# A Mamba-style scan with its output and gate turned to channels in rows, and the orders of five engines rewritten

## Chip, cores and metric

One NeuronCore of one Trainium2 chip. The metric is device time in microseconds (us) of the whole program, the median of several runs.

## The reference

For 32 sequences of 512 tokens with 256 channels, x becomes x + norm(attn(norm(x))) and then x + norm(ffn(norm(x))). All is fp32. The part called attn is a state-space scan:

```
q = rope(x @ W_in[:256].T); h = rmsnorm(q) * w
z, xBC, dt = split(h @ W_zxbcdt.T)            # 512, 768 and 8 columns
dt = softplus(dt + dt_bias)                   # 8 heads of 64 channels
x_ssm, B, C = split(silu(causal_conv4(xBC)))  # 512, 128 and 128
y = scan(x_ssm, dt, A, B, C) + D * x_ssm
y = rmsnorm(y * silu(z)) * w2
out = y @ W_out.T + q
```

The scan works in chunks: within a chunk y = (C B^T * decay) (x dt), and across chunks through a state of 128 x 64 for each head. The kernel uses chunks of 128 tokens. The part called ffn is a mixture of 16 experts of width 64 with a router, and a shared expert of width 512.

## The kernel before

The work of one sequence is cut into parts: p (first norm, q, rope, h by channel), a (projections, convolution, scan, output projection, residual), f (router, gates, ups, downs of the feed-forward) and g (final norm, store). An iteration of the loop does part a of sequence i, part p of sequence i+1, part f of sequence i-1 and the end of i-2, interleaved. Five engines run their own programs and meet only at semaphores. The order of each is written out by hand in the functions first, iteration, tail and drain of each engine's block: SP at 534 to 551, POOL (GpSimd) at 699 to 730, ACT (ScalarE) at 950 to 1002, DVE (VectorE) at 1336 to 1381, PE (TensorE) at 1659 to 1715. The loop runs iteration for i from 2 to 30; lead, first and iteration(1) stand ahead of it, tail, drain and last behind it.

PSUM has three banks for part a (apb), one for p (ppb), two for f (fpb) and two for the down projection (acc). PLANS lists in which order banks are filled, and which engine fills a name's reader and which frees it; slot() on PE waits until the bank's last user is done.

A product that must be nearly fp32 exact is done in split form: operands are rounded to a high part (fp32r) and a low rest, and split_mm (L1443) sends three matmuls for each block of 128 input channels: high x high, high x low and low x high. Matmuls within the scan take plain fp32 operands. narrow (L1492, L1494) does the same for few output columns, with tokens as the stationary operand: two matmuls for each block of 128 tokens and 128 channels.

The steps that the change touches, in order for chunk c of 128 tokens:

- project_z(c, n) puts z by token into PSUM, in halves a and b of 256 columns. The a half carries dt's 8 columns too (264). dt_bias_add(c) (L1112) reads them; silu_z (L855) writes zs, tokens in rows. decays, cumulate (L1518 to L1520) and evac_acs make the cumulated decays; SP stores them as rows to memory and loads them back replicated to all partitions (decay_rows), POOL masks them (L607), ACT takes their exp (exp_seg, L845), DVE multiplies them by C B^T (decay_CB, L1167), all in seg.
- x_by_token(c) transposes the convolved x (L1452). times_dt(c) makes xdt = x dt (L1159) and xD = D x (L1162).
- diagonal(c) (L1575): for each of 8 heads one matmul with seg (128 x 128) as the stationary operand and 64 columns of xdt streaming. Its output yd has tokens in rows.
- from_state(c) (L1560): C as the stationary operand, 512 columns of the state S streaming. state_part(c) (L1173) scales it by the decay of each token (ea). chunk_y(c) (L1191) adds the two. state(c) (L1567) and new_state(c) update S.
- gated(c) on POOL (L622, L623): y = (xD + chunk y) * zs.
- y_by_channel(c) transposes y in 4 pieces (L1452, ident with zs). evac_y (L867) and y_low (L1228) split it into yTh and yTl. square_y (L872) sums the squares of each token.
- project_out(t) is the output projection; mixed_out, add_x and norm_x1 (L881) finish the residual and normalise it for the feed-forward. ffn_by_channel (L1462, from xdt) transposes that at the start of the next iteration.

```
for h in range(HS):
    hs = slice(h * PD, (h + 1) * PD)
    ins = nc.tensor.matmul(b[:, hs], seg[:, c % 2, h, :], xdt[:, c % 2, hs], start=True, stop=True)
```

## Time and profile before

| | |
|---|---|
| median of 3 runs | 3193.36 us (3184.57 to 3193.8) |
| profiled execution | 3187.6 us; span from first to last instruction 3185.9 us |
| busy, of the span | PE 98%, PEld (weight loads) 85%, DVE 75%, ACT 61%, POOL 64% |
| share of PE in the chain that ended last | 95% |
| mean granted clock of TensorE | 0.989 of 2.4 GHz |

Busy time of PE is the union of records that overlap: a matmul's record ends when its last result is out, while the next has begun. The time that one costs is from its start to the next one's start. PEld are the loads of stationary operands, which can run ahead of the matmuls.

### The profile page before, as it was taken

Reading aid. Unit: us, or ns where it says so; the run is one execution under the profiler, and the core shown is the slowest. Engines: PE = TensorE matmul, PEld = TensorE weight load, DVE = VectorE, ACT = ScalarE, POOL = GpSimd, SP = SyncE. Lnnn points to the kernel's source line nnn. Section 1 sums busy time; section 2 is a strip of 40 time slices with the busy share of each in tenths; the row PEclk is TensorE's granted clock in tenths of the full one; section 3 lists DMA queues with packets and bytes.
Section 4 is the critical chain, followed back from the end, with each engine's and each line's share of the span. In section 5 each row is a group of like instructions: output and inputs, shape, how many; then the busy total and the mean of one; then the engine's idle time right before and its main releaser. Section 6 shows DMA issues by size and latency. Waiting matters only on the chain.

```text
span 3185.9 us, 62383 instructions
## 1 busy us (share of the span) xinstructions
PE 3112.3 (98%) x19648; PEld 2722.1 (85%) x19648; DVE 2394.2 (75%) x5104; ACT 1935.2 (61%) x4149; POOL 2031.2 (64%) x2311
## 2 busy tenths in 40 slices
PE   5899999999999999999999999999999999999997
PEld 4688888888888888888888888888888888888886
DVE  5877877777777777777777777778777777777763
ACT  5565666665666556666566666656656656665562
POOL 2477666677666676656676666776666776666764
PEclk7899999999999999999999999999999999999999
DMA  3123222222222222222122222222222222222222
GB/s 123 41 68 87 73 73 67 66 66 85 73 64 64 71 73 76 80 66 58 64 86 76 76 60 66 66 86 73 73 66 66 66 86 73 64 67 69 73 74 48
DMA packets 143433, 227.33 MB, mean 71 GB/s; under 512 B 18976, under 2 KB 88352, under 8 KB 143392
## 3 DMA queue, kind: packets, MB, share of 16 engines
q1 hardware_dynamic: 126496, 210.06, 20.1%
q0 software_dynamic: 16896, 16.78, 4.0%
q8 instruction: 20, 0.33, 0.0%
q14 instruction: 21, 0.17, 0.0%
HBM read 174.87 MB, written 35.13 MB: 66 GB/s over the span
## 4 chain that ended last, share of the span: by engine, by line
PE 95%; DVE 0%; POOL 0%; ACT 0%; issue 0%; ACTq 0%; DVEq 0%; POOLq 0%
PE fpb L1443 34%; PE apb L1443 20%; PE acc L1629 17%; PE apb L1575 7%; PE apb L1452 4%; PE ppb L1443 3%; PE apb L1560 3%; PE apb L1567 2%; PE ppb L1462 2%; PE apb L1547 1%; PE fpb L1492 1%; PE fpb L1462 1%; PE fpb L1494 1%; PE fpb L1608 0%; PE apb L1520 0%; PE apb L1519 0%
## 5 line engine op out<-in xcount | busy, mean ns | idle before, releaser
L652 POOL TENSOR_TENSOR hidL<-hid,hidH 128x512 fp32r<-128x512 f32 x384 | 544.9, 1419 | 234.8 <-ACT hidH L914 226.8
L1130 DVE SCALAR_TENSOR_TENSOR xc<-apb,cw,xc 128x511 f32<-128x511 f32 (+2 forms) x576 | 427.8, 747 | 63.9 <-ACT xc L827 35.9
L1629 PE MATMUL acc<-WDH,hidH 128*128 128x256 f32 x1536 | 456.7, 297 | 4.4 <-POOLq L654 4.4
L914 ACT CAST hidH<-hid 128x512 fp32r<-128x512 f32 x384 | 236.2, 615 | 341.9 <-POOL hid L647 283.6
L1629 PE MATMUL acc<-WDH,hidL 128*128 128x256 f32 x1536 | 431.4, 281 | 0.0
L1629 PE MATMUL acc<-WDL,hidH 128*128 128x256 f32 x1536 | 430.9, 281 | 0.0
L647 POOL TENSOR_TENSOR hid<-hid,cb 128x512 f32<-128x512 f32 x256 | 347.5, 1358 | 73.2 <-DVEq L1251 42.1
L1249 DVE TENSOR_TENSOR hid<-hid,fpb 128x512 f32<-128x512 f32 x384 | 261.1, 680 | 135.6 <-PE fpb L1443 132.3
L1443 PE MATMUL fpb<-fTh,UH 128*128 128x512 f32 x768 | 335.7, 437 | 0.0
L845 ACT ACTIVATE seg<-seg,acs 128x128 f32<-128x128 f32 x1024 | 313.6, 389 | 11.5 <-ACT cb L895 5.7
L1443 PE MATMUL fpb<-fTh,GH 128*128 128x512 f32 x768 | 318.6, 415 | 0.0
L1629 PEld LDWEIGHTS acc<-WDH,hidH 128*128 128x128 f32 x1536 | 289.9, 189 | 19.9 <-issue 7.4
L1443 PE MATMUL fpb<-fTh,GL 128*128 128x512 f32 x768 | 304.1, 396 | 0.0
L1443 PE MATMUL fpb<-fTh,UL 128*128 128x512 f32 x768 | 303.9, 396 | 0.0
L903 ACT ACTIVATE hid<-fpb 128x512 f32<-128x512 f32 x384 | 228.5, 595 | 123.2 <-PE fpb L1443 83.9
L1443 PE MATMUL fpb<-fTl,UH 128*128 128x512 f32 x768 | 302.5, 394 | 0.0
L1443 PE MATMUL fpb<-fTl,GH 128*128 128x512 f32 x768 | 302.5, 394 | 0.0
L1629 PEld LDWEIGHTS acc<-WDL,hidH 128*128 128x128 f32 x1536 | 290.1, 189 | 12.7 <-issue 7.2
L1629 PEld LDWEIGHTS acc<-WDH,hidL 128*128 128x128 f32 x1536 | 289.7, 189 | 0.0
L1575 PEld LDWEIGHTS apb<-xdt,seg 128*128 128x128 f32 x2048 | 246.7, 194 | 11.9 <-issue 6.6
L1575 PE MATMUL apb<-xdt,seg 128*128 128x64 f32 x2048 | 246.1, 274 | 2.9 <-DVE seg L1167 2.8
L1167 DVE TENSOR_TENSOR seg<-seg,CBs 128x1024 f32<-128x1024 f32 x128 | 198.4, 1550 | 43.6 <-ACT seg L845 34.1
(195 smaller groups left out, 8669.6 us busy)
## 6 DMA issues: line engine op xcount, KB each, us to landing
seg<-acs_row SPq DMA_DIRECT2D x128, 512.0 KB, 4.2
cb<-c_row SPq DMA_DIRECT2D x512, 128.0 KB, 2.9
xsP<-in_x SPq DMA_DIRECT2D x32, 512.0 KB, 3.6
xc<-qrot SPq DMA_DIRECT2D x32, 512.0 KB, 3.4
xc<-in_x SPq DMA_DIRECT2D x32, 512.0 KB, 4.3
out<-xc SPq DMA_DIRECT2D x32, 512.0 KB, 3.0
out<-xn POOLq DMA_DIRECT2D x32, 512.0 KB, 6.0
ZL_loaded<-in_wzx_t SPq DMA_DIRECT2D x2, 512.0 KB, 4.4
```

Source lines behind the costliest of these rows:

```text
L647: G.tensor_tensor(hid[:, j % 2, :], hid[:, j % 2, :], cb[:, r % 2, :], ALU.mult).then_inc(sem["routed_ready"], 1)
L652: own.do(G.tensor_tensor(hidL[:, j % 2, :], hid[:, j % 2, :], hidH[:, j % 2, :].bitcast(fp32), ALU.subtract))
L845: ins = A.activation(seg[:, c % 2, h, :], seg[:, c % 2, h, :], ACT.Exp, bias=acs[:, 0, c * HS + h:c * HS + h + 1])
L903: own.do(A.activation(hid[:, j % 2, :], way.bank(f"G{j}")[:], ACT.Silu))
L914: A.copy(hidH[:, j % 2, :], hid[:, j % 2, :]).then_inc(sem["hidden_high"], 1)
L1130: ins = V.scalar_tensor_tensor(xc[:, b, s:], src[:, 0:T - s], cw[:, b, TAPS - 1 - s:TAPS - s], xc[:, b, s:], ALU.mult, ALU.add)
L1167: V.tensor_tensor(seg[:, c % 2, :, :], seg[:, c % 2, :, :], CBs[:, c, :].unsqueeze(1).broadcast_to([P, HS, P]), ALU.mult).then_inc(sem["m_ ...
L1249: own.do(V.tensor_tensor(hid[:, j % 2, :], hid[:, j % 2, :], way.bank(f"U{j}")[:], ALU.mult))
L1443: ins = nc.tensor.matmul(dst, l, r, start=n == 0, stop=n == total - 1)
L1452: ins = nc.tensor.transpose(b[:, t * P:(t + 1) * P], src(t), ident[:])
L1575: ins = nc.tensor.matmul(b[:, hs], seg[:, c % 2, h, :], xdt[:, c % 2, hs], start=True, stop=True)
L1629: ins = nc.tensor.matmul(dst, l[:, w, tk], r[:, j, :], start=j == 0 and t % 2 == 0 and n == 0, stop=j == HB - 1 and n == 2, skip_group_che ...
```

## The change

The scan's output and z are kept with channels in rows and tokens along the row, so that y need not be transposed before the output projection.

- project_z(j) now has the weights of 128 channels as the stationary operand and 512 tokens streaming: four groups of six matmuls. dt gets a weight tile of its own, DTW, and project_dt, by narrow, for all 512 tokens. dt_bias_add takes all chunks at once.
- diagonal(c): 64 columns of xdt are the stationary operand and the 128 columns of seg stream. Even heads write partitions 0 to 63 and odd heads 64 to 127.
- from_state(c): four matmuls with a block of 128 columns of S as the stationary operand and C's 128 columns streaming.
- The decay of a token now varies along the row. own_rows on SP loads the decay rows of chunks 1 to 3 a second time, two heads to a block of channels, into own_decay (128 x 1536), which overlays xTh and xTl; row_exp on ACT takes their exp. state_part multiplies by them. ea is gone.
- xD = D x is made from xc in SBUF with D by channel (dcol).
- y_by_channel is gone. evac_y and y_low read zs. A single yTh/yTl pair is kept, which now has its own semaphores (yT_read, out_begun).
- The squares' sum runs over partitions now: square_y writes squares, sum_squares on DVE adds four blocks to one, squares_by_token on PE multiplies by a column of ones, squares_out copies to ssy.
- The orders of all engines and the plans of all stages are new, with more switches of ACT's function tables (exp_table, silu_table) in iteration: five pairs where there were three.

```diff
-            def project_z(c, n):
...
-                fill(name, split_mm(b[:, 0:cs.stop - cs.start], [(hTh[:, k, tk], hTl[:, k, tk], ZH[:, k, cs], ZL[:, k, cs])
-                                                                 for k in range(KD)],
-                                    sem["hT_read"] if c == NT - 1 and n == 1 else None))
+            def project_dt():
+                b = slot("dt")
+
+                pe.wait_ge(s_hT, 2)
+                pe.sem_inc(s_hT, -2)
+                fill("dt", narrow(b, hTh, hTl, DTW, HS))
+
+            def project_z(j):
+
+                name, lo = f"z{j}", j * P + (HS if j >= NB // 2 else 0)
+                cs = slice(lo, lo + P)
+                fill(name, split_mm(slot(name)[:], [(ZH[:, k, cs], ZL[:, k, cs], hTh[:, k, :], hTl[:, k, :])
+                                                    for k in range(KD)], sem["hT_read"] if j == NB - 1 else None))
...
-                fill(f"yo{c}", nc.tensor.matmul(b[:], xc[:, 5, c * P:(c + 1) * P], S[:], start=True, stop=True))
+                for j in range(NB):
+                    js = slice(j * P, (j + 1) * P)
+                    ins = nc.tensor.matmul(b[:, js], S[:, js], xc[:, 5, c * P:(c + 1) * P], start=True, stop=True)
+                fill(f"yo{c}", ins)
...
-                    hs = slice(h * PD, (h + 1) * PD)
-                    ins = nc.tensor.matmul(b[:, hs], seg[:, c % 2, h, :], xdt[:, c % 2, hs], start=True, stop=True)
+
+                    half = slice(h % 2 * PD, (h % 2 + 1) * PD)
+                    ins = nc.tensor.matmul(b[half, h // 2 * P:(h // 2 + 1) * P], xdt[:, c % 2, h * PD:(h + 1) * PD],
+                                           seg[:, c % 2, h, :], start=True, stop=True)
...
-            def y_by_channel(c):
-                b = slot(f"yT{c}")
-                pe.wait_ge(sem["yg_ready"], c + 1)
-                fill(f"yT{c}", transposes(b, lambda j: zs[:, c, j * P:(j + 1) * P], NB))
+            def squares_by_token(s):
+                b = slot(f"ss{s}")
+                for n in range(2):
+                    c = 2 * s + n
+                    pe.wait_ge(sem["qs_ready"], c + 1)
+                    ins = nc.tensor.matmul(b[:, n:n + 1], junk[n][:, 0:P], ones[:, 0:1], start=True, stop=True)
+                fill(f"ss{s}", ins)
...
+            def own_rows():
+
+                sp.wait_ge(sem["acs_stored"], 16)
+                for a in range(2):
+                    sp.dma_start(own_decay[a * PD:(a + 1) * PD, :, :],
+                                 rows(acs_row, [[0, PD], [2 * P, (NT - 1) * NB], [1, P]], (HS + a) * P)
+                                 ).then_inc(sem["ear_loaded"], 16)
...
+            def row_exp():
+                act.wait_ge(sem["ear_loaded"], 32)
+                A.activation(own_decay[:], own_decay[:], ACT.Exp).then_inc(sem["ear_ready"], 1)
...
+            def sum_squares(c):
+
+                dve.wait_ge(sem["sq_ready"], c + 1)
+                q = junk[c % 2]
+                own.do(V.tensor_tensor(q[:, 0:2 * P], q[:, 0:2 * P], q[:, 2 * P:4 * P], ALU.add))
+                V.tensor_tensor(q[:, 0:P], q[:, 0:P], q[:, P:2 * P], ALU.add).then_inc(sem["qs_ready"], 1)
```

The new order of PE in the loop (iteration; "if g" lines in place):

```
project_dt(); ffn_by_channel(0); project_x(4); ffn_by_channel(1); project_z(0); project_x(5); down(10)
logits(0); down(11); logits(1); cumulate(); project_x(0); gate(0); project_x(1); up(0); project_x(2)
gate(1); project_z(1); gate(2); project_x(3); up(1); gate(3); project_z(2); up(2); project_z(3); CB()
B_by_token(); down(0); x_by_token(0); up(3); x_by_token(1); down(1); combine_by_expert(); state(0)
gate(4); diagonal(0); x_by_token(2); down(2); up(4); down(3); gate(5); from_state(1); state(1); up(5)
gate(6); diagonal(1); from_state(2); state(2); up(6); down(4); diagonal(2); x_by_channel(0); gate(7)
x_by_token(3); up(7); down(5); squares_by_token(0); project_out(0); from_state(3); project_q(0)
diagonal(3); gate(8); down(6); up(8); x_by_channel(1); project_out(1); gate(9); project_q(1); down(7)
project_out(2); up(9); squares_by_token(1); gate(10); h_by_channel(0); project_out(3); down(8); up(10)
down(9); h_by_channel(1); gate(11); up(11)
```

## Rows read from the trace of the kernel before

**Rows 1.** Windows, one period: length, then busy PE, PEld, DVE, ACT, POOL, clock, DMA.
```profile
1500.00:1596.40 96.40, 96.36 (x616) 84.52 (x615) 74.14 (x160) 59.79 (x129) 63.31 (x74) 1.00 0.23 71
```
**Rows 2.** The chain of waits in order of time: start, length, piece, records.
```profile
1514.81 1.73 PE apb L1575 x16
...
1559.33 2.79 PE fpb L1443 x12
...
1588.54 0.71 PE apb L1443 x6
...
1611.20 1.73 PE apb L1575 x16
```
**Rows 3.** Timeline of PE: start, length of the group's records, line, form, records.
```profile
1503.85 1.05 PE L1547 MATMUL apb<-xc 128*128 128x128 f32 x8
1504.73 0.60 PE L1452 MATMUL apb<-ident,xc 128*128 128x128 f32 x4
```
**Rows 4.** Timeline of PE around diagonal(0).
```profile
1514.64 1.89 PE L1575 MATMUL apb<-xdt,seg 128*128 128x64 f32 x16
...
1516.66 0.39 PE L1443 MATMUL fpb<-fTl,UH 128*128 128x512 f32 x1
```
**Rows 5.** Timeline of PE around the transposes of y, chunk 0.
```profile
1528.25 0.60 PE L1452 MATMUL apb<-ident,zs 128*128 128x128 f32 x4
...
1528.92 0.39 PE L1443 MATMUL fpb<-fTl,GH 128*128 128x512 f32 x1
```
**Rows 6.** Timeline of PE around the router's product, first and last of 16 records.
```profile
1576.10 0.18 PE L1492 MATMUL fpb<-R,fTh 128*128 128x32 f32 x1
...
1577.69 0.26 PE L1494 MATMUL fpb<-R,fTl 128*128 128x16 f32 x1
1577.80 0.37 PE L1443 MATMUL apb<-ZH,hTh 128*128 128x264 f32 x1
1578.00 0.28 PE L1443 MATMUL apb<-ZL,hTh 128*128 128x264 f32 x1
```
**Rows 7.** Timeline of PE around from_state(1).
```profile
1517.83 1.02 PE L1560 MATMUL apb<-S,xc 128*128 128x512 f32 x2
1518.68 1.02 PE L1567 MATMUL apb<-xdec,Btok 128*128 128x512 f32 x2
```
**Rows 8.** Timelines of PE and DVE at the loop's boundary.
```profile
1566.83 0.40 PE L1443 MATMUL fpb<-fTh,UL 128*128 128x512 f32 x1
1567.27 0.36 PE L1443 MATMUL apb<-ZH,hTh 128*128 128x264 f32 x1
...
1566.47 0.69 DVE L1107 TENSOR_TENSOR hTl<-ppb,hTh 128x512 fp32r<-128x512 f32 x1
```
**Rows 9.** Timelines of PE and PEld around cumulate.
```profile
1589.09 0.30 PE L1518 MATMUL apb<-ad,upper 128*128 128x32 f32 x2
...
1589.55 0.41 PE L1520 MATMUL apb<-upper,ad 128*32 128x128 f32 x2
...
1590.22 0.39 PE L1443 MATMUL fpb<-fTl,GH 128*128 128x512 f32 x1
...
1589.20 0.30 PEld L1519 LDWEIGHTS apb<-ad,ones 128*128 128x128 f32 x2
1589.54 0.14 PEld L1520 LDWEIGHTS apb<-upper,ad 128*32 128x32 f32 x2
```
**Rows 10.** Groups of weight loads by form: busy us, mean ns of one, idle before.
```profile
L1518 PEld LDWEIGHTS apb<-ad,upper 128*128 128x128 f32 x64 | 10.1, 192 | 2.2 <-ACT xc L832 2.1
...
L1520 PEld LDWEIGHTS apb<-upper,ad 128*32 128x32 f32 x64 | 4.4, 109 | 1.3
```
**Rows 11.** Groups of ScalarE by form.
```profile
L765 ACT ACT_TABLE_LOAD x98 | 125.7, 1283 | 6.5 <-ACT hid L903 5.3
...
L855 ACT ACTIVATE zs<-apb 128x256 f32<-128x256 f32 x256 | 94.4, 382 | 25.0 <-PE apb L1443 13.7 <-ACT hid L903 8.1 <-DVE dr L1112 2.7
```
**Rows 12.** Timelines of ACT and PE at norm_x1(1) and ffn_by_channel(1).
```profile
1568.64 1.09 ACT L881 ACTIVATE xdt<-xc,nb,rstd 128x256 f32<-128x256 f32 x2
...
1570.64 0.60 PE L1462 MATMUL fpb<-ident,xdt 128*128 128x128 f32 x4
```

More of the change, by code:

```diff
@@ L242, in build @@
+            "drain": Plan({
                 "f": (
@@ new lines, in iteration @@
+                squares_by_token(0); project_out(0); from_state(3); project_q(0); diagonal(3); gate(8)
+                settled("m_ready"); down(6); up(8); x_by_channel(1); project_out(1); settled("xn_ready")
+                gate(9); project_q(1); down(7); settled("p_out_DVE"); project_out(2); up(9)
+                squares_by_token(1); gate(10); settled("a_out_DVE", "qs_ready"); h_by_channel(0)
+                project_out(3); settled("p_out_ACT"); down(8); settled("yl_ready"); up(10); down(9)
@@ new lines, in tail @@
+                logits(1); gate(0); B_by_token(); up(0); cumulate(); project_z(1); settled("ad_ready")
+                project_x(0); gate(1); project_x(1); gate(2); project_x(2); up(1); CB(); project_x(3); gate(3)
+                up(2); project_z(2); project_z(3); up(3); down(0); settled("acc_free"); x_by_token(0)
+                x_by_token(1); down(1); combine_by_expert(); gate(4); settled("c_ready"); state(0); up(4)
+                diagonal(0); gate(5); from_state(1); state(1); x_by_token(2); down(2); up(5); down(3); gate(6)
@@ new lines, in tail @@
+                state(2); diagonal(1); down(4); settled("xdec_ready"); from_state(2); up(6); gate(7); down(5)
+                x_by_token(3); from_state(3); up(7); settled("a_out_ACT"); diagonal(2); gate(8); down(6)
+                project_out(0); squares_by_token(0); up(8); gate(9); diagonal(3); project_out(1)
+                settled("m_ready"); down(7); up(9); gate(10); project_out(2); squares_by_token(1); down(8)
+                settled("a_out_DVE", "qs_ready"); up(10); project_out(3); gate(11); settled("f_out_ACT")
```

522 lines of the change are left out of this document (262 added, 260 removed).

## Prediction

> **What bounds the kernel now.** I read the busy table by windows first. One stretch of 96.40 us of the loop has TensorE busy for 96.36, VectorE for 74.14, ScalarE for 59.79 and GpSimd for 63.31, at the full clock (2.4 GHz) [rows 1]. The chain of waits gives the period: the first diagonal product of one iteration begins at 1514.81 and that of the next at 1611.20, so a sequence takes 96.4 us [rows 2]. 29 loop iterations make 2796 of the 3187.6 us. The profiled execution took 3187.6 (span 3185.9); the median of the three runs is 3193.36, which is 5.8 above it.
>
> "Busy" says little on TensorE, since its records overlap. I cost by start to start instead. A 512-column matmul of a split product takes 2.79/12 = 0.233 us, a 256-column one 0.71/6 = 0.118 [rows 2]. Full fp32 matmuls appear as two records each. With a 128-column stationary operand each record costs 0.111, whether 128 or 64 columns stream: B·C takes 0.88/8 = 0.110 [rows 3]; the diagonal product takes 1516.66 - 1514.64 - 0.233 = 1.79 for 16 records, 0.112 each [rows 4]. So the old diagonal product is bound by its weight loads. I add up TensorE's work per sequence, since nothing else fills the period.
>
> **What leaves and what comes, in TensorE time per sequence.**
>
> - *Transposes of y* (4 groups, L1452 with zs) go. One costs 1528.92 - 1528.25 - 0.233 = 0.44 [rows 5], so -1.76.
> - *z*: 24 matmuls of 256 columns and 24 of 264 become 24 of 512. Without the 8 extra columns (24 x 8 at 2.4 GHz is 0.08) the old ones take 48 x 0.118 = 5.66; in all 5.74 against 24 x 0.233 = 5.59: -0.15.
> - *dt* becomes a product of its own, of the same form as the router's: 16 matmuls with 128-column stationary operands. The router's take 1578.00 - 1576.10 - 0.12 = 1.78 [rows 6]. So +1.78: eight columns carried along almost free are now paid for with 16 weight loads.
> - *Sums of squares by token*: four fp32 matmuls with one streamed column, 8 records x 0.111 = +0.89.
> - *from_state*: one 512-column matmul, 1518.68 - 1517.83 = 0.85 [rows 7], becomes four of 128 columns, as B·C does at 0.88. Three times 0.03: +0.09.
> - *Loop boundary*: the last matmul of up(11) starts at 1566.83 and the first z at 1567.27 instead of 1567.06, because VectorE's second half of hTl runs from 1566.47 to 1567.16 [rows 8]. The exposed weight load after it adds 0.08. In the new order gate(11) and up(11), 2.8 us, follow h_by_channel(1) instead of 1.4, which covers this: -0.29.
>
> These sum to +0.56. All hang on the order holding, since TensorE has no gaps to fill.
>
> - *Diagonal product.* Before, 4 x 1.79 = 7.16. The stationary operand is now 64 columns of xdt and 128 columns stream. No row of before has two halves of the array in use, so I bound it. Above: one after another, a 128-column fp32 record streams twice, 256 columns at 2.4 GHz = 0.107, x16 = 1.71. Below: heads in different halves run side by side. Each head has two records in its own half, in order, so the last of one head overlaps the first of the next: 8.5 steps x 0.107 = 0.91. Weight loads permit this: one of 128 columns lasts 0.192 and one of 32 lasts 0.109 [rows 10], 0.00086 per column, so 64 columns issue about every 0.055, and 16 x 0.055 = 0.88.
> - *Entering and leaving a narrow stationary operand.* cumulate has one (L1520, 32 columns). From 1589.09 to 1590.22 less 0.233 is 0.90 for its six records, where 4 x 0.111 + 2 x 0.107 = 0.66 would do; the gap lies before and after L1520 [rows 9]. So 0.24 an excursion, four of them; with the wider exposed load I take 0.26. Bound below: nothing, as the 16-column combine transposes fit in ordinary time.
>
> I take side by side: 4 x (0.91 + 0.26) = 4.68, so -2.48. The row nearest to it is L1520: two loads there end 0.14 us after the first begins, against 0.30 for two wide ones [rows 9], and the array drains around them, as if it was set up differently for a narrow operand. Such a setup would be the one that has halves.
>
> A page bears on this from both sides. "TensorE: Matmul & The Clock Gate" of the Trainium skill, section "Part 3: Packing small matmuls", gives 2.38x for three column tiles; at that efficiency two tiles gain 1.59x, as an estimate, and the product would be 1.08 + 0.26. No run shows it yet.
>
> Sum: +0.56 - 2.48 = -1.92, a period of 94.5.
>
> **Other engines.** ScalarE loses eight silus of 0.382 [rows 11], the accumulator reads and one small exp; it gains four silus twice as long, an exp of 128x1536 (at most 6 x 0.382 = 2.3), and four table loads, five pairs a sequence for three, at 1.283 [rows 11] = 5.1. It ends near 65 to 66 of 94.5. VectorE gains about 3 (two short additions for each chunk, two copies), near 77. GpSimd keeps its work. All are below TensorE. SP gets two more row loads of 0.4 MB and issues decay_rows(1) ahead of decay_rows(0). Nothing that the first masks need stands behind the new loads, and from cumulate to diagonal(0) TensorE now has about 28 us of other work (14 projections, gates and ups of 1.4, and nine smaller groups); queued behind them are the prefetch of the next x, the combine rows and decay_rows(2), none needed within 10 us. The halves of x by channel, xTh and xTl, now share memory with own_decay: evac_xT(0) waits for chunk_y(2), which ends before it, as exp_seg(3) stands ahead of it on ScalarE.
>
> **Where lateness would show.** The tightest distance I find is the loop-carried one: project_out(3) to ffn_by_channel(1). Before, the second normalisation ends on ScalarE at 1568.64 + 1.09 = 1569.73 and its transposes start at 1570.64, so 0.9 in hand [rows 12]. The distance is 11.5 before, and after (down 1.42, up 1.40, down 1.42, transposes 0.44, gate and up 2.80, dt 1.78, transposes 0.44, xc4 1.40) it is 11.1: 0.5 left. The transposes head TensorE's in-order queue, so each further microsecond costs one per sequence. Next comes the new round trip square_y(3), sum_squares(3), squares_by_token(1), squares_out(1), root_y(1), mixed_out(1); its TensorE part stands 13 us after diagonal(3), and chunk_y, gated, gate(9), square, mixed_out(0) and rope(1) take about 11 of them. I allow 0.2 per sequence for such waits: -1.7.
>
> Over 31 sequences (the loop, iteration 1 and the tail; lead, first and drain I hold equal) that is -53, or 3135 against the profiled 3187.6. The runs lie on average 3 above it (two near 3193, one at 3184.6), and the after's median should as well: 3139.
>
> **Rivals.**
>
> 1. *The halves don't overlap.* Each diagonal product costs 1.71 + 0.26 = 1.97: 4 x 1.97 - 7.16 = +0.72, with +0.56 and no waits +1.28, x31 = +40: 3230, slower. This decides above 1.60 a product (there the sum with the 0.2 is zero). For it: every row of TensorE shows starts in order and at least a stream apart. Against it: the drain around L1520. Chance 0.19.
> 2. *Loads of a half aren't hidden behind the other half's matmul.* 16 x (0.055 + 0.107) + 0.26 = 2.85 each, +4.8 a sequence: 3340. Against it: the second load of L1520 is hidden. Chance 0.04. The same section of the Trainium skill speaks for this one: it says that a load overlaps a running matmul only in another row group, and all heads here use all rows.
> 3. *Lateness.* The halves overlap but the loop-carried chain or the squares' round trip keeps TensorE waiting 1 us or more a sequence: 3160 to 3190; at 1.9 the gain is gone. For it: 0.5 us in hand, ten table loads on ScalarE, more hops. Against: the before's orders show almost no idle time at all. Chance 0.10.
> 4. *Forecast*, 0.67. Its own range goes from 3105 (no drain cost: 4 x 0.26 x 31 = 32 less) to 3165 (the product at 1.4, +0.23 each, or waits of 0.9).
>
> **Numbers.** The range takes in the forecast's low end and rival 1 with the runs' spread: 3105 to 3235. That leaves out rival 2, parts of rivals 1 and 3, and a product cheaper still. Faster by over 0.3%, which is about what a measurement of this kernel tells from no change (10 us): 0.67 and most of rival 3, less a little for the ends: 0.71. Within 0.3%: 0.06. Slower: 0.23.
>
> **What would show it.** In the profile after: a period near 94.7; diagonal groups of 16 records in about 1.2 us with pairs of starts far less than 0.1 apart (rival 1: even steps of 0.107); gaps of 0.1 on both sides of each group; the dt group at 1.78; no idle time of TensorE before ffn_by_channel(1). A wait of TensorE on xdt's normalisation, or on the squares, would show rival 3. The forecast fails on the product's price before all else, since it alone turns the sign.

## The result and the profile after

The changed kernel takes 3356.43 us (median of 4, 3353.89 to 3359.7), the kernel before in the same job 3189.96: a ratio of 1.0524, 95% interval 1.0502 to 1.0545. The forecast was 3139 and faster. The profiled execution took 3357.49 us (span 3355.8).

The page of the kernel after, busy time and then the chain that ended last, by engine:

```profile
PE 3168.5 (94%) x19712; PEld 2702.9 (81%) x19712; DVE 2623.1 (78%) x5362; ACT 2138.6 (64%) x4015; POOL 2123.5 (63%) x2311
...
DVE 34%; PE 33%; ACT 10%; POOL 10%; issue 9%; DMA 3%; DVEq 0%; POOLq 0%; ACTq 0%; PEldq 0%; SPq 0%
```

TensorE, which held 95% of the chain before, now holds 33%, and VectorE as much: a new wait, not more work. A period was 96.4 us. It is now 102.1 in four iterations of five and 100.1 in the fifth. One of the short ones, the windows view of after (columns as in [rows 1]):

```profile
1052.50:1152.70 100.20, 95.67 (x619) 81.50 (x618) 81.19 (x167) 65.28 (x124) 66.52 (x72) 1.00 0.28 76
```

TensorE was busy for all but 0.04 us of its period in [rows 1]; here 4.5 are idle. ScalarE (65.3) is where the forecast put it, VectorE is 81.2 instead of 77. Who TensorE waited for over the whole run of after (total us, times, longest):

```profile
PE apb L1638 <- DVE xdec L1271: 71.0, 31, 2.3
PE ppb L1513 <- DVE xn L1112: 21.7, 32, 4.7
PE ppb L1497 <- DVE xTl L1092: 13.1, 10, 2.1
PE apb L1543 <- issue: 10.9, 30, 0.4
```

L1638 is squares_by_token and L1271 the second addition of sum_squares. Timeline of PE, after:

```profile
1081.99 0.40 PE L1497 MATMUL fpb<-fTh,GL 128*128 128x512 f32 x1
1082.31 1.09 PE L1629 MATMUL apb<-seg,xdt 128*64 128x128 f32 x16
1083.34 0.66 PE L1505 MATMUL apb<-ident,xc 128*128 128x128 f32 x4
...
1106.27 0.28 PE L1638 MATMUL apb<-ones,xc 128*128 128x1 f32 x2
1108.87 0.38 PE L1638 MATMUL apb<-ones,xdec 128*128 128x1 f32 x2 [2.33 <-DVE xdec L1271]
...
1140.65 0.40 PE L1497 MATMUL fpb<-fTh,UL 128*128 128x512 f32 x1
1141.41 0.25 PE L1543 MATMUL apb<-DTW,hTh 128*128 128x16 f32 x1 [0.36 <-issue]
```

Three things are to be read here. The 16 records of the diagonal product take 1082.31 to 1083.34, 1.03 us where before's take 1.70 (the 1.79 of [rows 4] takes in 0.08 of the step behind the group, from 1516.35 to 1516.66): the halves run side by side. Ahead of the group there is 0.09 more (0.32 from the last wide matmul instead of 0.233), and something behind it; experiment 1 gives the whole price. The sums of squares begin at 1106.27 and then stand for 2.3 us. And the loop's boundary has grown: 1140.65 to 1141.41 is 0.76, where [rows 8] had 0.44.

What VectorE did while TensorE stood, timelines of DVE and of POOL, after:

```profile
1103.49 0.62 DVE L1270 TENSOR_TENSOR xc<-xc 128x256 f32<-128x256 f32 x1 [0.24 <-DVE hid L1300]
1104.14 0.29 DVE L1271 TENSOR_TENSOR xc<-xc 128x128 f32<-128x128 f32 x1
...
1105.36 0.77 DVE L1263 TENSOR_TENSOR yTl<-zs,yTh 128x512 fp32r<-128x512 f32 x1 [0.33 <-DVE xdt L1219]
1106.06 1.49 DVE L1270 TENSOR_TENSOR xdec<-xdec 128x256 f32<-128x256 f32 x1
1107.58 1.24 DVE L1271 TENSOR_TENSOR xdec<-xdec 128x128 f32<-128x128 f32 x1
...
1105.54 1.72 POOL L634 TENSOR_TENSOR xD<-xD,xdt 128x512 f32<-128x512 f32 x1
1107.34 1.32 POOL L636 TENSOR_TENSOR zs<-zs,xD 128x512 f32<-128x512 f32 x1
```

The same two additions take 0.62 and 0.29 for chunk 0 and 1.49 and 1.24 for chunk 1, and each of the long ones ends just after a GpSimd instruction does (1107.55 after 1107.26, 1108.82 after 1108.66). Over the run, the 57 second additions that began with GpSimd idle took 0.291 to 0.294; the 71 that began under a running instruction had a median of 1.265, and their length follows what was left of it (correlation 0.98).

GpSimd waits too. Its 512-column operations that begin while VectorE has no operation under way on two SBUF sources take 1.28 (the low halves of hid, L665, median). The 157 on two sources that began under VectorE's seg<-seg,CBs, S<-S,el or y_low last 1.12 to 1.16 plus what was left of VectorE's operation (correlation 0.999): the 1.72 above began under y_low, which ends at 1106.13. So each engine's delay feeds the other's. Groups of DVE by form, after:

```profile
L1263 DVE TENSOR_TENSOR yTl<-zs,yTh 128x512 fp32r<-128x512 f32 x128 | 122.8, 959 | 22.7 <-DVE xdt L1219 17.2 <-ACT yTh L883 5.4
L1178 DVE TENSOR_TENSOR xD<-xc,dcol 128x512 f32<-128x512 f32 x128 | 106.2, 830 | 0.0
L1271 DVE TENSOR_TENSOR xdec<-xdec 128x128 f32<-128x128 f32 x64 | 82.7, 1292 | 2.2
...
L1201 DVE TENSOR_TENSOR own_decay<-apb,own_decay 128x512 f32<-128x512 f32 x96 | 65.6, 683 | 12.2 <-PE apb L1612 11.5 <-DVE ssy L1275 0.3 <-DVE xdt L1219 0.3
```

and of the kernel before:

```profile
L1178 DVE TENSOR_TENSOR S<-S,el 128x512 f32<-128x512 f32 x64 | 92.0, 1438 | 0.5 <-DVE xdt L1191 0.2
L1228 DVE TENSOR_TENSOR yTl<-apb,yTh 128x512 fp32r<-128x512 f32 x128 | 87.6, 685 | 18.1 <-ACT yTh L867 10.5 <-DVE xdt L1191 7.4
L1162 DVE TENSOR_TENSOR xD<-apb,dbc 128x512 f32<-128x512 f32 x128 | 86.9, 679 | 0.0
```

Where one source is a PSUM bank (apb), 512 columns take 0.68 us in both kernels. Where both are in SBUF they take 0.83, 0.96, 1.44 in the mean. y_low and xD were of the first kind and have become the second; sum_squares is new and of the second. With y_low this costs GpSimd as well: its operations that began under y_low have a median of 1.28 in the kernel before and of 1.71 after. The row S<-S,el was there to be read before the forecast.

That a VectorE operation with two SBUF inputs and a GpSimd instruction exclude each other is what the Trainium skill says ("SBUF — State Buffer", section "Who interferes with whom": such an instruction "contends with a GpSimd instruction that reads SBUF", the later one waits for the other's end, and tensor_reduce never contends on trn2). The trace agrees in the additions, in the waits of GpSimd and in the rows with one PSUM source; the reduction is tried below.

Last, the clock. Windows of after: from the start of the dt product (1039.62) on, and around the squares of the iteration before (TensorE is idle for 2.35 us within the third line, 2.48 busy of 4.83):

```profile
1039.62:1042.46 2.84, 2.84 (x23) 2.75 (x24) 0.49 (x1) 1.94 (x4) 2.62 (x6) 1.00 0.28 99
1042.46:1045.87 3.41, 3.41 (x12) 2.73 (x11) 1.08 (x4) 1.75 (x3) 2.57 (x3) 0.50 0.00 0
...
1003.50:1008.33 4.83, 2.48 (x23) 2.40 (x22) 4.46 (x6) 3.57 (x7) 2.91 (x2) 1.00 0.00 0
1008.33:1011.74 3.41, 3.41 (x19) 3.41 (x18) 2.41 (x4) 2.12 (x4) 2.41 (x3) 0.50 0.68 229
```

A granted clock of 0.50 is 1.2 GHz. Iterations of 102.1 us have two such stretches of 3.41 us, those of 100.1 none: one begins 0.7 to 1.8 us after TensorE's wait at the squares has ended, the other 1.9 to 3.0 us after the dt product has begun. Over the run they make 229.9 us, where the kernel before had 69.7, all of it outside 400 to 3000 us.

### The profile page after: what moved, and what is told of

Its sections match the earlier page's. It is cut to its first block, busy times and chain, and to the rows that moved or that the text cites. A ratio compares the mean times of both kernels' runs of the same rounds, so it can differ in the third digit from the quotient of the medians.

```text
span 3355.8 us, 63442 instructions
## 1 busy us (share of the span) xinstructions
PE 3168.5 (94%) x19712; PEld 2702.9 (81%) x19712; DVE 2623.1 (78%) x5362; ACT 2138.6 (64%) x4015; POOL 2123.5 (63%) x2311
## 4 chain that ended last, share of the span: by engine, by line
DVE 34%; PE 33%; ACT 10%; POOL 10%; issue 9%; DMA 3%; DVEq 0%; POOLq 0%; ACTq 0%; PEldq 0%; SPq 0%
PE apb L1497 10%; PE fpb L1497 8%; DVE xc L1144 6%; PE acc L1689 5%; ACT seg L856 4%; POOL hidL L665 3%; DVE hid L1300 3%; DMA out<-xn 3%; DVE xdec L1271 2%; ACT L777 2%; DVE st L1080 2%; DVE yTl L1263 2%; PE ppb L1497 2%; DVE xc L1270 2%; DVE S L1206 2%
## 5 line engine op out<-in xcount | busy, mean ns | idle before, releaser
L665 POOL TENSOR_TENSOR hidL<-hid,hidH 128x512 fp32r<-128x512 f32 x384 | 531.8, 1385 | 452.4 <-ACT hidH L928 436.8
L1144 DVE SCALAR_TENSOR_TENSOR xc<-apb,cw,xc 128x511 f32<-128x511 f32 (+2 forms) x576 | 430.7, 748 | 66.1 <-ACT xc L840 37.5
L1689 PE MATMUL acc<-WDH,hidH 128*128 128x256 f32 x1536 | 445.0, 290 | 3.1 <-POOLq L667 3.1
L1497 PE MATMUL fpb<-fTh,GH 128*128 128x512 f32 x768 | 327.7, 427 | 0.0
L917 ACT ACTIVATE hid<-fpb 128x512 f32<-128x512 f32 x384 | 228.3, 595 | 108.4 <-PE fpb L1497 94.2
L1497 PE MATMUL apb<-hTh,ZH 128*128 128x512 f32 x640 | 275.5, 430 | 3.5 <-ACT xc L845 3.5
L1497 PE MATMUL apb<-hTl,ZH 128*128 128x512 f32 x640 | 264.3, 413 | 0.0
L1497 PE MATMUL apb<-hTh,ZL 128*128 128x512 f32 x640 | 263.9, 412 | 0.0
```

Of the source, the lines that this page charges most:

```text
L665: own.do(G.tensor_tensor(hidL[:, j % 2, :], hid[:, j % 2, :], hidH[:, j % 2, :].bitcast(fp32), ALU.subtract))
L917: own.do(A.activation(hid[:, j % 2, :], way.bank(f"G{j}")[:], ACT.Silu))
L1144: ins = V.scalar_tensor_tensor(xc[:, b, s:], src[:, 0:T - s], cw[:, b, TAPS - 1 - s:TAPS - s], xc[:, b, s:], ALU.mult, ALU.add)
L1497: ins = nc.tensor.matmul(dst, l, r, start=n == 0, stop=n == total - 1)
L1689: ins = nc.tensor.matmul(dst, l[:, w, tk], r[:, j, :], start=j == 0 and t % 2 == 0 and n == 0, stop=j == HB - 1 and n == 2, skip_group_che ...
```

## The experiments

All ratios are to the kernel before on the same chip; its median lay between 3186.3 and 3190.5 in every job. "Period" is from cumulate to cumulate.

**1. The diagonal product alone, on the kernel before.** `b1_halves` turns it round with heads in alternating halves, `b2_one_half` puts heads 0 to 3 in one half and 4 to 7 in the other. Both leave the layout of y as it comes, so the output isn't the reference's.

```diff
-   ins = nc.tensor.matmul(b[:, hs], seg[:, c % 2, h, :], xdt[:, c % 2, hs], start=True, stop=True)
+   half = slice(h % 2 * PD, (h % 2 + 1) * PD)        # b2_one_half: h // 4
+   ins = nc.tensor.matmul(b[half, h // 2 * P:(h // 2 + 1) * P], xdt[:, c % 2, h * PD:(h + 1) * PD],
+                          seg[:, c % 2, h, :], start=True, stop=True)   # b2_one_half: h % 4
```

> The kernel before with the diagonal product alone turned round: 64 columns of xdt as the stationary operand, seg streaming, even and odd heads in the two halves of the partitions. Nothing behind it is adapted, so y has the wrong layout: only the time is read. In the trace of the changed kernel such a product takes 1.03 us for its 16 records, 1.1 with what it adds around it, against 1.79. If that price holds by itself and TensorE is still the bound: 4 x 0.69 x 32 = 88 us less, about 3102. If the price in the changed kernel only came from TensorE having waited before it, no change: 3190.

> As the one before, but heads 0 to 3 go to one half and heads 4 to 7 to the other, so that neighbours in the order share a half (the layout of y is again not the reference's). If the gain comes from two halves running side by side, this has none: 15 steps of 0.107 and 0.2 around them, 1.8 to 1.9 a product, 3190 to 3205. If it comes from the smaller stationary operand (loads of 64 columns), this is as fast as the alternating one, about 3102.

`b1_halves`: 3129.56 (3127.3 to 3132.4), 0.9816 (0.9796 to 0.9836), periods of 94.2 and 94.6. `b2_one_half`: 3177.14, 0.9966 (0.9955 to 0.9976), period 96.1. The product in each, timelines of PE, first of `b1_halves`:

```profile
1392.20 0.28 PE L1443 MATMUL apb<-ZH,hTl 128*128 128x256 f32 x1
1392.41 1.09 PE L1575 MATMUL apb<-seg,xdt 128*64 128x128 f32 x16
1393.43 0.51 PE L1443 MATMUL fpb<-fTh,UH 128*128 128x512 f32 x1
1393.78 0.40 PE L1443 MATMUL fpb<-fTl,UH 128*128 128x512 f32 x1
```

and of `b2_one_half`:

```profile
1412.72 1.58 PE L1575 MATMUL apb<-seg,xdt 128*64 128x128 f32 x16
1414.23 0.50 PE L1443 MATMUL fpb<-fTh,UH 128*128 128x512 f32 x1
```

1.02 against 1.51: most of the gain comes from heads in different halves next to each other, and it is worth 57 us by itself. The change's central idea holds; the loss comes from the rest. Both expectations missed in size. In `b2_one_half` the starts within a half are 0.109 apart, as expected, but the seven steps around the one change of half (heads 3 and 4) are 0.055 in the mean, which I had not counted. And 3102 was too low because the price of 1.1 left out what stands behind the group. Counted as in [rows 4], up to the second matmul behind it, the product costs 1393.78 - 1392.20 - 0.118 - 0.233 = 1.23, where [rows 4] has 1.79. That is 0.56 less, four times 2.24, and the shorter period is 2.22 below before's 96.4. The longer one has 0.4 more, at two steps inside the down and z products. The changed kernel's product by the same count costs 1.22.

**2. The additions.** `a1_reduce` lets VectorE sum the four blocks with one operation (ACT writes the squares so that the four to be summed lie side by side). `a2_no_adds` leaves the sum out and copies one column in its place.

```diff
-   own.do(V.tensor_tensor(q[:, 0:2 * P], q[:, 0:2 * P], q[:, 2 * P:4 * P], ALU.add))
-   V.tensor_tensor(q[:, 0:P], q[:, 0:P], q[:, P:2 * P], ALU.add).then_inc(sem["qs_ready"], 1)
+   V.reduce_sum(q[:, 0:P], q.rearrange("p (n j) -> p n j", j=NB), AX.X).then_inc(sem["qs_ready"], 1)
...
-   A.activation(junk[c % 2].rearrange("p (j n) -> p j n", j=NB), zs[:, :, c * P:(c + 1) * P], ACT.Square
+   A.activation(junk[c % 2].rearrange("p (n j) -> p j n", j=NB), zs[:, :, c * P:(c + 1) * P], ACT.Square
```

> The changed kernel with sum_squares as one reduction instead of two additions (the squares are written interleaved, so that it reads four neighbours for each sum); the same orders, the same result. Theory: VectorE's additions with both sources in SBUF wait until GpSimd's running instruction ends, take 7.1 us a sequence where 2.8 would do, and this makes VectorE late for squares_by_token, project_q(1) and h_by_channel(1). A reduction has one source and should not wait: about 0.65 x 4 = 2.6 a sequence, the wait at squares_by_token(0) falls from 2.4 to under 0.5, and the time to 3200 to 3260. Rival, the orders themselves are too tight (ScalarE's table loads, chunk y of chunk 2): the waits move elsewhere, 3330 or more.

> The changed kernel without the sum over the four blocks of squares: a copy of one column stands in for both additions, so the mean square is that of a quarter of the channels. The bound of what sum_squares can cost. Theory: 3190 to 3240, with no wait at squares_by_token(0). Rival, tight orders: 3320 or more.

`a1_reduce`: 3198.28 (3195.29 to 3204.34), 1.0038 (1.0026 to 1.005), period 96.05, and 97.6 in every third or fourth iteration; 97.1 us at half speed. `a2_no_adds`: 3187.77, 1.0007 (0.9995 to 1.0019). The edit of `a1_reduce`, the reduction and the order in which ScalarE writes the squares, carries 158 of the 167 us. Both times lie just below the range given for them. Groups of DVE and waits of TensorE, `a1_reduce`:

```profile
L1270 DVE TENSOR_REDUCE xdec<-xdec 128x128 f32<-128x512 f32 x64 | 43.0, 672 | 0.1
...
PE apb L1504 <- DVE xD L1178: 17.6, 30, 4.0
PE ppb L1512 <- DVE xn L1112: 11.8, 32, 4.7
```

The reduction takes 0.67 whether GpSimd runs or not (0.669 to 0.689 over 128). Per sequence that is 2.7 us of VectorE, against 7.1 for the additions, which alone would be 2.8. But VectorE's busy time of a period falls only from 81.2 to 79.3: in the new phase S<-S,el takes 1.72 in the mean for 1.24, seg 1.71 for 1.38 and y_low 1.22 for 0.96, all on two SBUF sources. Laid side by side at full clock, the periods of 100.14 (after) and 96.04 differ in TensorE's waits: squares_by_token(0) +2.47, project_q(1) +1.30 (for x_low(1), which VectorE does behind sum_squares(2)), h_by_channel(1) +0.46, four of 0.06 to 0.12, and x_by_token(2) -0.55.

**3. Where the squares are read, and whether they are awaited.** `a3_ss_later` moves squares_by_token(0) behind project_out(0); `a6_not_awaited` keeps both additions, but TensorE takes the fourth block of the squares, as ScalarE left it, and leaves out the others.

```diff
-   squares_by_token(0); project_out(0); from_state(3); ...          # a3_ss_later
+   project_out(0); squares_by_token(0); from_state(3); ...
...
+   dve.sem_inc(sem["qs_ready"], 1)                                  # a6_not_awaited
    own.do(V.tensor_tensor(q[:, 0:2 * P], ...))
-   V.tensor_tensor(q[:, 0:P], q[:, 0:P], q[:, P:2 * P], ALU.add).then_inc(sem["qs_ready"], 1)
+   own.mark(V.tensor_tensor(q[:, 0:P], q[:, 0:P], q[:, P:2 * P], ALU.add))
```

> The changed kernel with one step of TensorE's order moved in the steady iteration: the sums of squares by token of the first half stand behind project_out(0) (1.4 us of work) instead of ahead of it. Theory (VectorE's additions finish late because they are held up by GpSimd; the place in the order only decides how much of it TensorE sees): the 2.4 us that TensorE waits there shrinks to about 1.0, project_out(0) is ready on its own, and the period falls by about 1.4 from 102.1, perhaps 2 if a stretch at half speed shortens: 3290 to 3320. Rival (the place in the order is the whole fault): the wait vanishes and with it the stretches at half speed, period 96 to 97, 3200. Rival (the wait is for something else that comes at the same time): no change, 3357.

> The changed kernel with both additions on VectorE kept in their places, but TensorE takes only the fourth block of the squares and doesn't wait for them (three blocks are left out of the sum). This parts the additions' time on VectorE from the wait for their result. Theory (both count: the result comes late, and 7 us of VectorE time make x_low, norm_q and others behind them late): the 2.4 us wait goes, the period falls to about 98 and the stretches at half speed get rarer; 3220 to 3270. Rival A (only the round trip of the squares costs): 3190, as without the additions. Rival B (only VectorE's load costs): 3350.

`a3_ss_later`: 3297.12, 1.0331 (1.0306 to 1.0356), periods from 98.8 to 102.0, near what the theory had; at full clock 1.3 us less than after's 100.1. The wait has become two, of 0.8 at the squares and of 1.06 at from_state(3). `a6_not_awaited`: 3357.07, 1.0527 (1.0508 to 1.0545), no gain at all: my theory gave 3220 to 3270, and rival B, VectorE's load alone, was right. Waits of TensorE, `a6_not_awaited`:

```profile
PE apb L1613 <- DVEq L1055: 61.1, 30, 2.1
PE ppb L1514 <- DVE xn L1112: 23.5, 33, 4.7
PE ppb L1498 <- DVE xTl L1092: 22.7, 18, 2.6
```

The 2.3 us wait has moved, as one of 2.1, to from_state(3), whose bank is that of xt3, and times_dt(3), which frees it, stands right behind sum_squares(1) on VectorE. The wait named in the table was only the first of several for the same late engine.

**4. The suspected cost put into the kernel before.** `b3_adds` puts the two additions, on data that nobody reads, behind chunk_y four times a sequence; `b4_reduce` one reduction in each place.

```diff
    dve.sem_inc(sem["y_ready"], 1)                                   # end of chunk_y
+   for _ in range((0, 2, 1, 1)[c]):
+       own.do(V.tensor_tensor(ysp[:, 0:2 * P], ysp[:, 0:2 * P], ysp[:, 2 * P:4 * P], ALU.add))
+       own.do(V.tensor_tensor(ysp[:, 0:P], ysp[:, 0:P], ysp[:, P:2 * P], ALU.add))
...
+       own.do(V.reduce_sum(ysp[:, 0:P], ysp.rearrange("p (n j) -> p n j", j=4), AX.X))   # b4_reduce
```

> The kernel before with the suspected cost put in: the same two additions (256 and 128 columns, both sources in SBUF) four times a sequence, on data that nobody reads, in VectorE's order right behind chunk_y (twice behind that of chunk 1, once behind 2 and 3). Nobody waits for their result, only for what stands behind them on VectorE. Theory (VectorE has no room in time around the chunks, though it is busy for 74 of 96.4 us only, so work of its own there delays TensorE): 2.8 us of work and up to 4 us of waiting for GpSimd become 2 to 5 us of period: 3250 to 3340. Rival (the orders of before have room on VectorE, and only the changed kernel's orders have not): within 0.3% of 3190.

> The kernel before with one reduction (128 x 512 to 128 x 128, about 0.68 us) in each of the four places where the additions stood in the run before, on the same data that nobody reads. Own time on VectorE 2.7 us a sequence, as that of the additions alone (2.8). Theory (the additions cost by waiting for GpSimd, the reduction doesn't wait): 2.7 of VectorE time instead of 6.2, period 96.4 to 97.5, 3190 to 3225. Rival (any 2.7 us of work at these places makes VectorE late): 3303 as with the additions.

`b3_adds`: 3302.87, 1.0359 (1.0344 to 1.0374), period 99.65. `b4_reduce`: 3204.41, 1.0051 (1.0036 to 1.0067), period 96.5 and, in a third of the iterations, 96.9. Groups of DVE, `b3_adds`:

```profile
L1199 DVE TENSOR_TENSOR ysp<-ysp 128x128 f32<-128x128 f32 x128 | 101.0, 789 | 4.4
L1198 DVE TENSOR_TENSOR ysp<-ysp 128x256 f32<-128x256 f32 x128 | 96.5, 754 | 24.1 <-DVE xdt L1191 23.0
```

and `b4_reduce`:

```profile
L1198 DVE TENSOR_REDUCE ysp<-ysp 128x128 f32<-128x512 f32 x128 | 87.8, 686 | 24.0 <-DVE xdt L1191 22.9
```

This is the plainest pair. The own time is nearly the same (the additions 0.29 + 0.43 with GpSimd idle, four times: 2.9; the reduction 2.7). With its waiting the first comes to 6.2 us a sequence. The first costs 116 us and the second 18, in a kernel whose VectorE was busy for 74 of 96.4 us.

**5. GpSimd's instructions cut in four.** `a7_pool_pieces` is the changed kernel with GpSimd's 512-column operations on two sources in pieces of 128 columns.

```diff
-   own.do(G.tensor_tensor(hidL[:, j % 2, :], hid[:, j % 2, :], hidH[...].bitcast(fp32), ALU.subtract))
+   for k in range(4):
+       ks = slice(k * P, (k + 1) * P)
+       ins = G.tensor_tensor(hidL[:, j % 2, ks], hid[:, j % 2, ks], hidH[...ks...].bitcast(fp32), ALU.subtract)
+   own.do(ins)                                                      # and so for xdec, xD, zs, hid
```

> The changed kernel with GpSimd's 512-column operations on two sources (xdec, the two of the gate, the combine product, the low halves of hid) cut in four of 128 columns each, VectorE's work untouched. Theory (a VectorE operation with two SBUF sources waits until the GpSimd instruction that is running ends): the wait is cut to what is left of a short one: the second addition falls from a median of 1.27 us under GpSimd's work to 0.3 to 0.7, the product with D and the state's product fall towards their 0.7, and TensorE's wait before the squares falls from 2.4 to under 1; 3200 to 3290, if GpSimd itself gets no more than some per cent slower. Rival (GpSimd keeps the memory as long as its queue has work, or the two share its bandwidth, whatever the length of an instruction): the additions stay at 1.3 and the time at 3357 or more.

3589.19, 1.1256 (1.1236 to 1.1276). The size of the waits is as the theory had it, the time is not. Groups of DVE and POOL:

```profile
L1282 DVE TENSOR_TENSOR xdec<-xdec 128x128 f32<-128x128 f32 x64 | 23.2, 362 | 2.2
...
L675 POOL TENSOR_TENSOR hidL<-hid,hidH 128x128 fp32r<-128x128 f32 x1536 | 736.9, 511 | 436.9 <-ACT hidH L939 421.3 <-POOL hidL L675 15.5
```

The second addition fell from 1.29 to 0.36, so what holds VectorE up is the rest of the running instruction. But four pieces take 4 x 0.511 = 2.04 where one took 1.39 (undisturbed, 4 x 0.46 = 1.84 and 1.28), GpSimd's work grew from 2123 to 2599 us, and TensorE now waited for it: 154.9 us over the run before down products and 73.9 for xdec.

**6. The product with D.** `a5_xt_free` (on `a1_reduce`) frees the bank and sets GpSimd's xdec going before xD; `a8_xd_first` keeps the new place of these two and issues xD ahead of xdt (for chunks 1 to 3 ahead of the wait for the bank as well). Both wait for VectorE's own write before they signal.

```diff
+   own.do(ins)                      # ins: xdt = xt * dt
+   free("a", f"xt{c}")
+   dve.sem_inc(sem["xdt_ready"], 1)
    ins = V.tensor_tensor(by_block(xD[:, c % 2, :]), xc[:, 0:NB, ...], dcol[...], ALU.mult)   # a8_xd_first: ahead
-   free("a", f"xt{c}", ins)
```

> The kernel with one reduction in place of the two additions (3198), and one more edit: the bank of the transposed x is given free after its product with dt, its last reader, and not after the product with D, which no longer reads it. Theory (the product with D, now with both sources in SBUF, is held up and TensorE's next transposes wait for the bank, 17.6 us over the run): these waits go and the period falls by up to 0.5 from 96.05; 3184 to 3192. Rival (the lost time turns into the next wait behind it, as for the masked scores or xdec): 3198 as before.

> The kernel with the reduction (3198), and the product with D issued ahead of xdt instead of behind it for chunks 1 to 3, so that the instruction that sets GpSimd's xdec going has nothing with two SBUF sources right behind it. In the form that gave the bank and xdt free first, GpSimd took xdec before the product with D began, which then took 1.16 us in the mean instead of 0.83, and the whole 60 us more. Theory (who starts first holds the other up: GpSimd's start is set by VectorE's signal): the product falls to 0.7 to 0.9, no wait of TensorE on it, 3180 to 3200. Rival (the loss of that form came from the pause for the own write, not from who comes first): 3240 to 3260 again, since that pause is kept.

3258.01, 1.0205 (1.0185 to 1.0226), and 3254.62, 1.0204 (1.0189 to 1.0219): 60 and 56 us worse than what they were meant to mend. xD takes 1.155 in the mean in the first and 1.197 in the second (chunks 1 to 3; chunk 0's takes 0.691), against 0.823 in `a1_reduce`. The longest begin under other GpSimd instructions than xdec: under the gate's product (1.72, 30 times) in the first, under hidL's (1.76, 30 times) in the second. So the waits turn on which instruction of the two engines starts first, and two edits of a few tenths changed that for the worse. My account for it (that xdec's signal alone decides) failed in the second, which met the rival's 3240 to 3260. Whether the pause for the own write or the new phase does it stays open.

**7. xD taken off VectorE for two chunks.** `a9_fused` (on `a1_reduce`) adds D x to the bank of the diagonal product in four operations with one PSUM source; `a11_fused_first` also issues the other two xD first.

```diff
+   if c < 2:                                                        # chunk_y
+       for j in range(NB):
+           ins = V.scalar_tensor_tensor(xD[:, c % 2, j * P:(j + 1) * P], xc[:, j, c * P:(c + 1) * P], dcol[:, j:j + 1],
+                                        way.bank(f"yd{c}")[:, j * P:(j + 1) * P], ALU.mult, ALU.add)
```

> The kernel with the reduction (3198), and for chunks 0 and 1 no product with D and no chunk copy or sum on VectorE: four operations of 128 columns take x times D plus the PSUM bank of the diagonal product straight to xD, one source in PSUM; GpSimd adds the part from the state (chunk 1) and nothing for chunk 0. It computes the same. VectorE loses two products with D (1.4 alone, 1.7 as they run) and two 512-column operations (1.4), and gets 8 of about 0.2 each; GpSimd loses one addition of 1.42. Theory (VectorE's lateness around the chunks is what the changed kernel pays for, and sources in PSUM are not held up): period 95.0 to 95.7, 3165 to 3190. Rival (the rest of the loss lies elsewhere: the loop's end, the tail and the dt product): 3195 to 3200.

> Both edits together on the kernel with the reduction: products with D gone into the chunk sums for chunks 0 and 1, and ahead of xdt for chunks 2 and 3. Theory: as the better of the two, 3160 to 3190, below the kernel before. Rival: the signals move GpSimd's instructions under other operations of VectorE and the gain is lost there, 3200 or more.

3197.67, 1.0029 (1.0019 to 1.004), and 3197.29, 1.0028 (1.0018 to 1.0038): nothing gained. TensorE's wait of 0.55 on xD is gone, and 0.25 at the squares, 0.08 before x_by_channel(1) and steps of 0.05 to 0.13 took its place; the full-clock period is 96.01 for 96.05. So the rival's 3195 to 3200 came: VectorE's busy time fell by 3.3 us a period (79.3 to 76.0) and the period by 0.04.

**8. The dt product and the clock.** On `a1_reduce`, in the steady iteration: `a12_dt_second` puts ffn_by_channel(0) ahead of the dt product, `a13_dt_halves` cuts it in two halves with ffn_by_channel(0) and project_x(4) between them.

```diff
-   project_dt(); ffn_by_channel(0); project_x(4); ffn_by_channel(1)
+   ffn_by_channel(0); project_dt(); project_x(4); ffn_by_channel(1)                    # a12_dt_second
+   project_dt(0); ffn_by_channel(0); project_x(4); project_dt(1); ffn_by_channel(1)    # a13_dt_halves
```

> The kernel with the reduction (3198), and in the steady iteration the dt product behind the first four transposes of the next FFN input instead of ahead of them. Theory (the fall of TensorE's clock follows the idle time at the loop's end together with 1.78 us in which only 8 and 16 columns stream): with the transposes between them the stretches at half speed in the loop (24 us, seven of 3.4, each costing 1.5) go or get fewer: 3185 to 3195. Rival (the dt product alone brings the fall): no change in clock, 3198; and VectorE starts its iteration 0.4 us later, at most 3210.

> The kernel with the reduction (3198), and the dt product of the steady iteration cut in two halves of 0.89 us, with four transposes and the 1.4 us of project_x(4) between them, as the router's two halves stand apart. Theory (a long stretch of narrow products lets the clock fall): no half speed in the loop, -10 us, against it dt_bias_add waiting 1.8 us longer at the head of VectorE's order, which has room there: 3186 to 3200. Rival (VectorE's start is tight too): 3220 to 3260, with waits of TensorE on the convolution.

`a12_dt_second`: 3216.86, 1.0089 (1.0073 to 1.0104), more half speed in the loop (37.5 us for 23.9) and 25.1 us of waits for norm_x1; that is outside both the theory and the rival. `a13_dt_halves`: 3189.25, 1.0008 (0.9998 to 1.0018), and none between 400 and 3000 us, at a period of 96.2. In `a1_reduce` all seven half-speed stretches between 400 and 3000 us began 2.6 to 3.2 us after the dt product did; with the product in two parts they are gone. Why only every third or fourth iteration has one, though all do the same work, stays open.

**9. Three attempts to go below before.** On `a9_fused`: `a14_fused_order` with dt second and norm_q(1) ahead of mixed_out(1) on VectorE; `a15_fused_halves` with the dt product's halves as in `a13_dt_halves`; `a16_fused_halves_near` with only ffn_by_channel(0) between them.

```diff
-   h_low(0); mixed_out(1); norm_q(1); up(10)                                           # VectorE, a14_fused_order
+   h_low(0); norm_q(1); mixed_out(1); up(10)
...
+   project_dt(0); ffn_by_channel(0); project_dt(1); project_x(4); ffn_by_channel(1)    # TensorE, a16_fused_halves_near
```

> The kernel with the reduction and with D x in the chunk sums for chunks 0 and 1 (3198), with the dt product behind the first transposes and norm_q(1) ahead of mixed_out(1) on VectorE. It computes the same. Theory: the wait of 0.45 before h_by_channel(1) goes (-13 us) and some half-speed stretches too (-5 to -10): 3170 to 3185, below the kernel before. Rival (mixed_out(1) late makes the next iteration's norm_x1(1) late and TensorE waits before ffn_by_channel(1)): 3195 to 3215.

> The kernel with the reduction, with D x taken into the chunk sums for chunks 0 and 1 (3198), and the dt product of the steady iteration in two halves around ffn_by_channel(0) and project_x(4), as in the run that came to 3189. It computes the same. Theory (the two edits are independent: the first leaves periods of 96.0 and some of 97.6, the second takes the stretches at half speed): 3180 to 3190, at or just below the kernel before. Rival (VectorE's start, 1.8 us later, costs here): 3195 to 3210.

> The same, with only the four transposes of ffn_by_channel(0) (0.44 us) between the halves of the dt product and project_x(4) behind both. Theory (the fall of the clock comes with the stretch of narrow streams and transposes at the head of the iteration as a whole, not with its being in one piece): some half-speed stretches of 3.4 us come back, 3190 to 3200. Rival (any cut of the dt product is enough): no half speed between 400 and 3000 us, 3178 to 3190.

`a14_fused_order`: 3348.61, 1.05 (1.0485 to 1.0514). Waits of TensorE:

```profile
PE fpb L1524 <- ACT xdt L899: 69.6, 31, 2.9
```

norm_q(1) made VectorE wait for GpSimd's root (55.8 us over the run), mixed_out(1) came that much later, and with it norm_x1 of the next iteration: the loop-carried chain of the forecast, with 2.25 us of wait in an iteration where 0.5 was in hand, and 243.7 us at half speed. The rival named the mechanism, but its 3195 to 3215 were far too low.

`a15_fused_halves`: 3183.75 (3179.02 to 3188.44), 0.9986 (0.9977 to 0.9995), the only whole kernel not above before; the difference is smaller than the 0.3% that the prediction called measurable. `a16_fused_halves_near`: 3192.64, 1.0021 (1.0012 to 1.003), with 20.5 us of half speed back in the loop. A cut alone isn't enough; what lies between the halves matters. A period of `a15_fused_halves`:

```profile
1500.00:1596.10 96.10, 95.36 (x619) 81.78 (x619) 76.89 (x169) 68.06 (x125) 65.08 (x72) 1.00 0.29 80
```

## Why the prediction was wrong

- *Diagonal product*: the mechanism was right and the size nearly so. 1.22 to 1.23 each against 1.17, 2.24 a period saved against 2.48, and `b1_halves` shows it worth 57 us alone. Rival 1 is out. So is rival 2: by the page of the Trainium skill named there ("TensorE: Matmul & The Clock Gate", "Part 3: Packing small matmuls") a load overlaps only in another row group, which would have made it 2.85; 16 records in 1.03 with all rows in use leave no room for that, and the measurement decides.
- *The small terms*: right. dt 1141.41 to 1143.18, 1.77 for 1.78; z four blocks of 1.38 to 1.40; squares_by_token 0.37 where nothing is late, and 0.08 on the matmul behind it, for 0.45; from_state 0.81 to 0.89.
- *Loop boundary*: wrong by 0.5. The forecast took 0.29 off, as the wait there was VectorE's, and left a plain step of 0.23. With that wait covered, the row names issue (0.36, in every iteration), and the step from up(11) to the next product is 0.76. What the engine does in this time no run shows.
- *"VectorE gains about 3, near 77"*: this is the step that failed. It costed additions, y_low and xD as if their length was their own. With both sources in SBUF they last until GpSimd's instruction ends, so the additions took 7.1 for 2.8, and the engine stood at 81. Even with the additions gone it stood at 79 (`a1_reduce`). Neither the sum nor a rival named this wait.
- *Lateness*: "I allow 0.2 per sequence" came to 4.5 us of TensorE idle (0.36 of it the boundary's) plus the clock. The forecast had the right place, the squares' round trip (rival 3, chance 0.10), but priced it at 1 to 2 us and looked for slack at the wrong scale: `b3_adds` shows that 6.2 us more of VectorE's time around the chunks lengthens even before's period by 3.25, and `b4_reduce` that 2.7 fit in for 0.1, in some iterations 0.5. Neither 74 of 96 busy nor the 11 us of distance said that there was no room just there. And `a6_not_awaited` shows that it isn't the squares' result but all that stands behind the additions on VectorE.
- *The clock*: not in the forecast. Two stretches at half speed in most iterations, 160 us more of them over the run; one costs 1.0 us of a period of after and 1.5 of `a1_reduce`. Shown: they follow the wait at the squares and the dt product, and go when the waits go and the product is cut. Why 1.78 us of dt does it and the router's two parts of 0.9 don't was not measured further than `a16_fused_halves_near`.
- *What is left between 3139 and 3198*: the full-clock period of `a1_reduce` is 96.05 for the sum's 94.5. Boundary +0.5, h_by_channel(1) +0.4, xD +0.55 and the product +0.2 come to 1.65, so 0.1 is over. The forecast had allowed 0.2 for waits, so 1.35 x 31 = 42 us of the 59 are the period's, and half speed, 27 us more of it than before's, gives some 10; the last 7 are not traced (1 of them is a slip, 3135 and 3 being 3138).

## What to carry to other kernels

Before costing a VectorE operation, look where its sources are: with both in SBUF and a busy GpSimd, add the rest of the running GpSimd instruction (and to GpSimd's the rest of VectorE's); a change of layout that moves a source from PSUM to SBUF, or adds a tensor_tensor, pays it each time; in these runs a reduction or a PSUM source avoided it. A wait in the table is for a late engine, not for one result: take the named result away and see if the wait moves. An engine's share of busy time tells nothing about the room at one place; put a dummy of the suspected length there (`b3_adds`, `b4_reduce`) and measure.

## What the runs showed of the hardware

- A 128x128 addition within SBUF on VectorE: 0.29 us with GpSimd idle, 1.27 (median) when it runs instructions of 1.3 to 1.7 us, 0.43 when it runs pieces of about 0.5. The other way, a 128x512 GpSimd operation on two sources takes 1.28 us, and 1.12 to 1.16 plus the rest of VectorE's operation when it begins under one with two SBUF sources. A reduction of 128x512 to 128x128 within SBUF: 0.67 to 0.69 in all cases.
- 16 records of the diagonal product: with stationary operands of 64 columns in alternating halves and 128 streamed columns 1.03 us; with four heads in one half and then four in the other, 1.51; with 128-column stationary operands and 64 streamed, 1.70. With the steps around the group: 1.23, 1.71 and 1.79.
- TensorE fell to 1.2 GHz for 3.41 us at a time, in some iterations and not in others: 1.8 to 3.2 us after the start of 1.78 us of products that stream 8 and 16 columns, and 0.7 to 1.8 us after the end of a wait of 2.3 us.
- Four GpSimd operations of 128 columns take 2.04 us where one of 512 takes 1.39; undisturbed 1.84 and 1.28.
